# Rotation product, row statistics, gate and scatter of the first expert layer in one stage

## The reference

```python
x = x + _L0_gnn_ref(_layernorm(x), edge_weight, src, dst)   # layernorm(x) @ m, m = product of 100000 rotations
x = x + _L0_ffn_ref(_layernorm(x)[None], gate_w, gate_b, w1, b1, w2, b2)[0]

# in _L0_ffn_ref, with 8 experts and room for C = 977 rows in each:
logits = x @ gate_w + gate_b
probs = softmax(logits); idx = argmax(probs); prb = probs[idx]
pos = (cumsum(one_hot(idx)) * one_hot(idx)).sum(-1) - 1      # place in the expert's room
buf = zeros((E, C, D)).at[idx, where(pos < C, pos, C)].set(x, mode='drop')
```

## Time and profile before

| | us |
|---|---|
| median of 3 runs (7909.3 to 7910.01) | 7909.55 |
| the profiled execution, its time | 7921.19 |
| the profiled execution, its span | 7919.4 |
| busy in the span: PE / DVE / ACT / POOL | 5157.7 / 3609.7 / 3195.4 / 4682.5 |
| mean granted clock of TensorE, share of full speed | 0.743 |

### The profile page before, as it was taken

One profiled execution on the slowest core, in us unless ns is written; L12 is line 12 of the kernel. 1 busy time (PEld: TensorE's weight loads), 2 busy tenths in 40 slices (PEclk: granted clock), 3 DMA queues, 4 the chain that ended last, 5 costly groups with the idle time before them and its releaser, 6 DMA issues. The chain is left out here.

```text
span 7919.4 us, 115948 instructions
## 1 busy us (share of the span) xinstructions
PE 5157.7 (65%) x22196; PEld 4061.3 (51%) x22197; DVE 3609.7 (46%) x8810; ACT 3195.4 (40%) x8284; POOL 4682.5 (59%) x4875
## 2 busy tenths in 40 slices
PE   2689867777645555779734344566677566676796
PEld 2566544454434444579734344345456345455795
DVE  7634467777820000453500000466666566667533
ACT  2533244444343433333333333244444344444432
POOL 5032277777567777125277777677774777773253
PEclk9779977777777777779755555577778777777698
DMA  2432144444233333222311111344443344442324
GB/s 61 176 78 83 48 120 117 115 117 116 83 100 108 109 109 108 66 78 70 100 28 28 28 28 26 91 115 115 115 114 83 103 115 115 114 114 66 106 69 137
DMA packets 417887, 726.44 MB, mean 92 GB/s; under 512 B 129365, under 2 KB 278315, under 8 KB 414167
## 3 DMA queue, kind: packets, MB, share of 16 engines
q0 software_dynamic: 208256, 503.58, 23.6%
q1 hardware_dynamic: 202475, 208.74, 8.5%
q10 hardware_dynamic: 6508, 8.01, 0.3%
HBM read 596.63 MB, written 123.54 MB: 91 GB/s over the span
## 5 line engine op out<-in xcount | busy, mean ns | idle before, releaser
L1017 POOL DMA_INDIRECT g_rows<-table,src_idx x2326 | 2218.0, 954 | 710.0 <-issue 709.4
L1292 PE MATMUL g_p_win<-g_rows,g_hot 128*128 128x264 f32 (+1 forms) x4704 | 1502.2, 477 | 44.5 <-issue 41.4
L1292 PEld LDWEIGHTS g_p_win<-g_rows,g_hot 128*128 128x128 f32 x4704 | 1069.1, 238 | 305.3 <-issue 94.0
L1182 ACT ACTIVATE g_hot<-iota,near 128x128 f32<-128x128 f32 x2352 | 720.7, 386 | 411.7 <-PE g_p_win L1292 375.7
L1017 POOL DMA_INDIRECT g2p_rows<-rows,src_idx x771 | 736.3, 955 | 235.2 <-issue 235.2
L1017 POOL DMA_INDIRECT gcnp_rows<-table,src_idx x771 | 734.8, 953 | 235.5 <-issue 235.5
L1098 DVE TENSOR_TENSOR g_rows<-g_rows,g_p_w 128x1792 f32<-128x1792 f32 x336 | 679.0, 2021 | 27.0 <-ACT g_rows L1210 2.7
L1201 ACT ACTIVATE g_resets_f<-fwd_reset 128x112 f32 (+3 forms) x168 | 54.8, 326 | 1176.1 <-DVE g_b L1069 1061.3
L1249 PE MATMUL g_p_turn<-slide,g_a 128*8 128x128 f32 (+1 forms) x168 | 59.0, 351 | 715.6 <-DVE g_a L1057 715.6
L1105 DVE TENSOR_TENSOR agg<-agg,g2p_p_out 128x256 f32 x112 | 42.1, 417 | 943.3 <-PE g2p_p_out L1254 943.3
L1105 DVE TENSOR_TENSOR agg<-agg,gcnp_p_out 128x64 f32 x112 | 20.3, 221 | 957.0 <-PE gcnp_p_out L1254 957.0
(11 more groups left out here) (831 smaller groups left out, 10986.2 us busy)
## 6 DMA issues: line engine op xcount, KB each, us to landing
g_stage<-table SPq DMA_DIRECT2D x3328, 1.0 KB
g_rows<-table,src_idx POOLq DMA_INDIRECT x2326
g2p_stage<-rows SPq DMA_DIRECT2D x1664, 1.0 KB
gcnp_stage<-table SPq DMA_DIRECT2D x1664, 0.2 KB
back<-agg SPq DMA_DIRECT2D x7, 1792.0 KB, 34.9
rows<-r_row SPq DMA_DIRECT2D x98, 128.0 KB, 3.0
gcn_row_in<-back SPq DMA_DIRECT2D x14, 896.0 KB, 7.3
c_row<-back SPq DMA_DIRECT2D x14, 896.0 KB, 13.5
```

The lines of the kernel that those rows point to most:

```text
L1017: gp.indirect_dma_start(rows[:, s, j, 0:width + H], None, table, bass.IndirectOffsetOnAxis(g.src_idx[:, at:at + 1], 0)).then_inc(got[s], 16)
L1182: last = nc.scalar.activation(hot[:, j, :], g.iota[:, :], ACT.Square, scale=-1.0, bias=g.near[:, bass.ds(c * J + j, 1)])
L1292: last = nc.tensor.matmul(p_win[:, 0:W], hot[:, j, :], rows[:, s, j, :], start=(j == 0), stop=(j == J - 1))
```

## The change

`x_plus_product` and `front` are gone. One function, `product_front`, does the work of both in a single stage. `STEPS` is 61 and the loops run over t from 0 to 66. In step t an engine works at tile t of the product and at tile t - 12 (`LAG`) of the gate. Statistics become `GroupNorms`: scale and shift are worked out for each group of seven tiles (six DVE instructions "spread", a square root on ACT "root", two DVE instructions "fit"), since the gate part needs them while the product goes on. The turned tile of the gate part is copied from PSUM to `rt` by DVE, no longer by ACT. The PSUM buffers `p_x`, `p_r` and `p_pos` are single, `out` and `p_log` double. `first` and `tmp` become double. `g.mt` moves from a buffer of its own into a part of `agg` that lies behind `row`. The sum of the counts, the penalties and everything behind the stage are unchanged. `room_known` stands on ACT before the first tile of the product.

```diff
-def x_plus_product(nc, g, name, rhs, bias=None):
...
-def front(nc, g, name, w, bias, top2, softmax, prefetch, room_known=None):
+def product_front(nc, g, name, rhs, w, bias, prefetch, room_known):
+    NG, LAG = NT // GROUP, 12
...
+        p_x, p_r = ph.ps("p_x", [P, 2, P]), ph.ps("p_r", [P, 2, P])
+        out = [ph.ps(f"out{s}", [P, D]) for s in range(2)]
+        norms = GroupNorms(nc, g, ph)
+        STEPS = NT + LAG
+        ending = lambda t, after: (t - after) % GROUP == GROUP - 1 and 0 <= t - after < NT
+        group_of = lambda t, after: (t - after) // GROUP
+        CHOOSE, COUNT, PLACE = LAG + 1, LAG + 3, LAG + 4
...
             @block.scalar
+                def feed(t):
+                    if t >= 2:
+                        ac.wait_ge(fed_turned, t - 1)
+                    normalised(nc, g, xn[:, t % 2, :], t).then_inc(fed, 1)
+                def copy_fed(t):
+                    ac.wait_ge(fed_turned, t + 1)
+                    if t >= 2:
+                        ac.wait_ge(summed, t - 1)
+                    nc.scalar.activation(xt[:, t % 2, :, :], p_x[:, :, :], ACT.Identity).then_inc(fed_copied, 1)
+                room_known(ac)
+                feed(0)
+                feed(1)
+                copy_fed(0)
+                for t in range(STEPS + 6):
+                    if t + 2 < NT:
+                        feed(t + 2)
+                    if 0 <= t - LAG + 2 < NT:
+                        normalise(t - LAG + 2)
+                        if (t - LAG + 2) % GROUP == 0:
+                            name_rows((t - LAG + 2) // GROUP)
+                    if t + 1 < NT:
+                        copy_fed(t + 1)
+                    if ending(t, CHOOSE + 1):
+                        exps(group_of(t, CHOOSE + 1))
+                    if ending(t, 1):
+                        norms.root(ac, group_of(t, 1))
             @block.tensor
+                def turn_fed(t):
+                    pe.wait_ge(fed, t + 1)
+                    if t >= 1:
+                        pe.wait_ge(fed_copied, t)
+                def product(t):
+                    pe.wait_ge(fed_copied, t + 1)
+                    if t >= 2:
+                        pe.wait_ge(added, t - 1)
+                def turn(t):
+                    pe.wait_ge(normal, t + 1)
+                    if t >= 1:
+                        pe.wait_ge(copied, t)
...
+                turn_fed(0)
                 pe.wait_ge(loaded, 32)
                 pe.wait_ge(tri_ready, 2)
+                for t in range(STEPS + 6):
+                    if t + 1 < NT:
+                        turn_fed(t + 1)
+                    if t < NT:
+                        product(t)
+                    if 0 <= t - LAG + 1 < NT:
+                        turn(t - LAG + 1)
+                    if 0 <= t - LAG < NT:
+                        multiply(t - LAG)
+                    if ending(t, COUNT):
+                        positions(group_of(t, COUNT))
             @block.vector
+                def take(t):
+                    x = g.x[:, t, :]
+                    dv.wait_ge(summed, t + 1)
+                    V.tensor_tensor(x, x, out[t % 2][:, :], ALU.add).then_inc(added, 1)
+                    dv.wait_ge(added, t + 1)
+                    norms.tile(t)
+                def copy(t):
+                    dv.wait_ge(turned, t + 1)
+                    if t >= 2:
+                        dv.wait_ge(multiplied, t - 1)
+                    V.tensor_copy(rt[:, t % 2, :, :], p_r[:, :, :]).then_inc(copied, 1)
...
+                for t in range(STEPS + 6):
+                    if 0 <= t - LAG < NT:
+                        copy(t - LAG)
+                    if t < NT:
+                        take(t)
+                    if ending(t, 0):
+                        norms.spread(dv, group_of(t, 0))
+                    if ending(t, 2):
+                        norms.fit(dv, group_of(t, 2))
+                    if ending(t, CHOOSE):
+                        choose(group_of(t, CHOOSE))
+                    if ending(t, PLACE):
+                        put_group(group_of(t, PLACE))
...
-        front(nc, g, "r0", a["L0_ffn_gate_w"], a["L0_ffn_gate_b"], False, True, wt.first_two, lambda gp: gp.wait_ge(g.filled, 16 * g.fills))
+        product_front(nc, g, "r0", g.mt, a["L0_ffn_gate_w"], a["L0_ffn_gate_b"], wt.first_two, lambda eng: eng.wait_ge(g.filled, 16 * g.fills))
...
-        g.mt = sb("mt", [P, 2, D])
+        g.mt = g.agg_wide[:, :, :].rearrange("p t w -> p (t w)")[:, NT * RW:NT * RW + 2 * D].rearrange("p (k d) -> p k d", k=2)
-        x_plus_product(nc, g, "l0g", g.mt[:, :, 0:D])
```

More of the change, by code:

```diff
@@ L2162, in name_rows @@
                         ac.wait_ge(ops, 1)
[L2163 to L2169, removed]
+                    nc.scalar.activation(row[:, n, :, D:D + 1].rearrange("p t a -> p (t a)"), ids[:, tiles_of(n)], ACT.Identity).then_inc(named, 1)
@@ L2195, in _ @@
                 mm = nc.tensor.matmul
+                def turn_fed(t):
+                    pe.wait_ge(fed, t + 1)
+                    if t >= 1:
+                        pe.wait_ge(fed_copied, t)
+                    for k in range(2):
+                        last = nc.tensor.transpose(p_x[:, k, :], xn[:, t % 2, k * P:(k + 1) * P], g.ident[:, :])
+                    last.then_inc(fed_turned, 1)
+                def product(t):
+                    pe.wait_ge(fed_copied, t + 1)
+                    if t >= 2:
+                        pe.wait_ge(added, t - 1)
+                    for k in range(2):
+                        last = mm(out[t % 2][:, :], xt[:, t % 2, k, :], rhs[:, k, :], start=(k == 0), stop=(k == 1))
+                    last.then_inc(summed, 1)
                 def turn(t):
@@ L2285, in _, with put_group @@
+                    V.tensor_tensor(tmp[:, s, :, :], sc, over_e(best[:, gs]), ALU.subtract).then_inc(less, 1)
+                def put_group(n):
+                    s, last, gs = n % 2, n == NG - 1, tiles_of(n)
                     dv.wait_ge(counted, n + 1)
[L2286 to L2288 removed]
+                    where = by_tile(p_pos[:, :, :])
+                    ch.do(V.tensor_scalar(over[:, :, :], where, CAP - 0.5, OUT, ALU.is_ge, ALU.mult))
@@ L2289, in _ @@
                     ch.do(V.tensor_tensor(place[:, :, :], where, region[:, :, :], ALU.add))
-                    if not top2:
-                        ch.do(V.tensor_tensor(place[:, :, :], place[:, :, :], over[:, :, :], ALU.add))
-                    for k, chosen_one in enumerate((first, second)[:K]):
-                        ch.do(V.tensor_tensor(eq[:, :, :], chosen_one[:, :, :], place[:, :, :], ALU.mult))
-                        ch.do(V.tensor_reduce(out=slot[:, :], in_=eq[:, :, :], axis=AX.X, op=ALU.add))
-                        if last:
-                            ch.do(V.tensor_tensor(slot[:, :], slot[:, :], invalid[:, :], ALU.add))
-                        V.tensor_copy(put[:, k, gs], slot[:, :]).then_inc(put_ready, 1)
-                        dv.wait_ge(put_ready, K * n + k + 1)
@@ L2299, in _ @@
[L2299 to L2305 removed]
+                    ch.do(V.tensor_tensor(place[:, :, :], place[:, :, :], over[:, :, :], ALU.add))
@@ new lines, in put_group @@
+                    ch.do(V.tensor_tensor(eq[:, :, :], first[:, s, :, :], place[:, :, :], ALU.mult))
+                    ch.do(V.tensor_reduce(out=slot[:, :], in_=eq[:, :, :], axis=AX.X, op=ALU.add))
+                    if last:
+                        ch.do(V.tensor_tensor(slot[:, :], slot[:, :], invalid[:, :], ALU.add))
+                    V.tensor_copy(put[:, gs], slot[:, :]).then_inc(put_ready, 1)
+                    dv.wait_ge(put_ready, n + 1)
+                    dv.wait_ge(exped, n + 1)
```

191 lines of the change are left out of this document (49 added, 142 removed).

## The result

| | before | after |
|---|---|---|
| median, us | 7909.78 (7909.14 to 7913.7, 6 runs) | 7940.73 (7934.13 to 7944.05, 6 runs) |
| ratio after to before | | 1.0037, 95% interval 1.0024 to 1.005 |
| the profiled execution's span, us | 7919.4 | 7942.1 |
| next stage's first load (SP, `e_xin`), us from the span's start | 477.12 | 508.74 |

The change makes the kernel 31 us slower, 0.4%. I had said 7934, 24.6 us slower. The stretch that the change touches is 31.6 us longer; behind it both kernels do the same, and the profiled execution of before happened to lie above its median there. They took 23 us more than the kernel before beside them, so the loss is 23 to 31 us.

A forecast was written before the change was run, and what follows sets the result against it. Before, PE bounds the product stage and, at 1.2 GHz, is busy through most of the gate stage. 362.6 + 95.9 + 20.9 + 0.3 + 22.0 = 501.7 against 477.1, 24.6 us longer: 7934 us, range 7904 to 7958.

The forecast's parts named there:

- The head: Stage start: ACT waits for the DRAM-table clears, so work starts at 345.4 instead of 317.0, 28.4 us lost.
- Steps with the product alone: First 12 tiles, before gate work: 1.9 us to the first product plus 15.3 us, as before.
- Mixed steps: 37 tiles, t = 12 to 48, product and gate together: PE and DVE wait in turn, 95.9 us.
- I take 18%: Mixed steps: share of time with TensorE at 1.2 GHz, from a later stage, raising 90.9 to 95.9 us.
- Steps with the gate alone: Last 12 tiles: 15.6 us at 1.3 each, plus one choose, put, fit and positions, 5.3; together 20.9 us.
- The end: Last choose to the next stage's first load: 22.0 us instead of 24.1, as the scatter queue is gone.
- ACT and its tables: Merged stage: ACT doesn't bind; ten more table loads, 1.28 us each, cost nothing, falling where PE waits for choose or put.
- Rival 1: Mixed steps: DVE and PE run past each other, only DVE's queue counts, 74 us; 7907 in all; chance 0.16.
- Rival 2: Head: the clears land sooner and are no wait, 28.4 us less, 7906 alone; chances 0.05, 0.04 with Rival 1.
- rival 3: Mixed steps: TensorE stays at 1.2 GHz, 128 us instead of 95.9, 7966 in all; chance 0.08.
- my own case: Merged stage: PE and DVE wait for each other in a loop, from +8 to +42 us; chance 0.62.
- Rival 4: Merged stage: ACT's table loads are not covered, 19 us more, 7953 in all; chance 0.05.

The follow-up runs named there:

- e1: Changed kernel with only ACT's wait for the DRAM-table clears moved from the first tile to its first write into row (t = 10): 7939.86 us.
- e2: As e1, with PE's and DVE's waits for the gate weights also moved to their first use: 7927.17 us.
- e3: Changed kernel with the exponential of the scores replaced by a plain copy, removing 10 of 11 table loads: 7940.26 us.
- e5: Changed kernel with the second copies (p_r to rt) back on ACT instead of DVE: 7914.04 us.
- e9: e5 with the exponential of the scores replaced by a plain copy, as in e3: 7907.54 us.
- e4: Changed kernel with DVE's choose and put cut into pieces of two instructions, exponential, positions and put one or two steps later: 7920.69 us.
- e8: Changed kernel with the pieces of e4, the moved waits of e2, and the gate part 19 tiles behind instead of 12: 7896.29 us.
- e6: Changed kernel with unread matmuls on PE, 5 behind the product at choose and 4 at put: 7932.81 us.

## Why the prediction was right, point by point

**The head.** Predicted 28.4 us lost, start at 345.4; it was 27.7 and 344.69. The load of the gate weights, which I took as hidden, is a gate of its own (e1), 1 us behind the clears; it cost next to nothing in after, where the first product started at 347.55 and I had 347.3. What I hadn't seen is that half of the loss would stay with the wait at its first real use (e2), because of ACT's queue.

**Steps with the product alone.** First mixed step predicted at 362.6; the first product followed by transposes of the gate side starts at 362.07.

**Mixed steps.** This term was too small: 95.9 us predicted, 101 measured (362.1 to DVE's last addition at 463.19). Of its parts, the plain step was 1.75 and measured 1.70, and the reason given for it was wrong: I had PE and DVE wait for each other in a loop, and the trace shows PE without a gap and DVE waiting. That the number came near is luck, since PE's own work alone came to 1.67. The bursts were right in place: choose takes 2.4 us on DVE (399.04 to the copy at 401.46), and PE stands for 2.13 of it. What failed is "I take 18%" of the time at 1.2 GHz, from the earlier trace rows. It was 46% in after (0.77 from 363 to 453); but the same mixed part had 0.89 and 0.85, 22% and 30%, in e1 and e3, and took 97 to 98 us there:

```profile
363.00:453.00 90.00, 73.07 (x432) 62.30 (x432) 60.97 (x218) 60.75 (x128) 23.71 (x25) 0.89 0.17 60
```

So this share isn't one number for this kernel, and mine lay below all three. The 0.29 in the sum isn't explained in the prediction; it fits 1 - 2.46 / 3.45, the part by which a tile is shorter at the full clock. With 46% the sum would have given 105. Some of the difference to 101 comes from put: at 1.2 GHz PE is busy with the product through most of it (to 412.53, where put ran from 410.99 to 412.80) and stops for 0.80 us, where e1 at the full clock had 1.91, as predicted. So "PE idle over 2 us behind every choose and put" was right for choose alone. The group period was 20.4 in the profile and 18.8 to 20.5 in e1 and e3, and the 17 to 19 that I had named holds for three of the eight groups of e1 and e3 and for none of after; PEclk, which I had put at 0.8 to 1, was outside in after and inside in the other two.

**Steps with the gate alone.** 20.9 and 0.3 predicted, 23.3 measured (463.19 to the last choose at 486.53), and 23.3 in e1 and e3 too. A step took 1.27 at 1.2 GHz, where I had 1.3. The fault is in the count: with `PLACE` at t = `LAG` + 4 behind a group's last tile, puts fall at t = 22, 29, 36 and 43 in the mixed part and at 50 and 57 here, and the sum has one here, six in all for seven groups. The missing one, 1.9 in the prediction's own price, is about the 2.1 that this term is short. The two puts, and PE's wait for DVE's copy behind each:

```profile
467.87 0.22 DVE L2265 TENSOR_SCALAR r_over<-r_p_pos 128x56 f32<-128x56 f32 x1 [0.92 <-PE r_p_pos L2190]
...
470.22 0.66 PE L2172 MATMUL r_p_r<-slide,agg 128*128 128x128 f32 x2 [1.36 <-DVE r_rt L2236]
...
480.67 0.22 DVE L2265 TENSOR_SCALAR r_over<-r_p_pos 128x56 f32<-128x56 f32 x1 [1.16 <-PE r_p_pos L2190]
...
483.01 0.66 PE L2172 MATMUL r_p_r<-slide,agg 128*128 128x128 f32 x2 [1.29 <-DVE r_rt L2236]
```

(One `positions`, at t = 49, also belongs here and not in the mixed part, where the sum has five; that moves 0.4 from one term to the other.) **The end:** 22.0 predicted, 22.2 measured (508.74 - 486.53).

**ACT and its tables.** Cost at nothing was right (e3). It holds only while another stop covers the loads; in e5 that cover is gone, and e9 shows the price, 5 to 6.5 us. The Trainium skill (ScalarE: Activation LUTs, What ACT_TABLE_LOAD costs) gives a drain of about 1.38 us with each switch. The traces here show none. After has, on ACT's timeline:

```profile
403.90 0.38 ACT L2112 ACTIVATE r_xt<-r_p_x 128x256 f32<-128x256 f32 x1 [1.08 <-PE r_p_x L2155]
404.30 1.28 ACT L478 ACT_TABLE_LOAD   x1
405.60 0.30 ACT L478 ACTIVATE r_g_std<-r_g_var,r_g_eps 128x7 f32<-128x7 f32 x1
```

The load starts 0.02 us behind the copy's end, and the root starts 0.02 us behind the load: 1.28 us is all. It is the same for the exponential where it waits for nothing else (e5: load at 393.90, exponential at 395.21).

**The rivals.** Rival 1 (only DVE's queue counts, a group of 14.0) didn't happen, and e4 shows why: it needs DVE's work in pieces, and then a group does take 14.9. Rival 2 (the clears are no wait) and rival 3 (1.2 GHz throughout) are out by the rows above; the truth lay between 3 and my own case, nearer to my own. Rival 4 is out by e3. The missing 7 us of the profile are the mixed part (5, by the clock) and the put left out of the count (2); in e1 and e3 some 3 us were missing, of which the mixed part is 1 to 2.

**What was luck.** The sign rested on the head, which was read to within 1 us. From the head's end to the next stage's first load I had 156.3 us (501.7 - 345.4) against 160.1 before (477.12 - 317.0), so a merged stage 4 us faster than the two apart. It was 160 (e3) to 164 (after), so level with the two or 4 us slower. On the work itself the prediction named the wrong side, by 4 to 8 us, and the loss of 28 us ahead of it kept that from showing in the sign.

**Where the gain of merging went.** With the copies left on ACT the merged stage needs 134.7 us from ACT's first tile to the next stage's first load (478.77 less 344.07, in e5), where the two stages took 160.1 (477.12 less 317.0). So merging is worth 25 us. The copies by DVE take all of it back (508.74 - 344.69 = 164.0 in after, 160 in e3), and the wait at the head, 28 us, is then the loss. The copies were undone by themselves (e4, e5). The head was undone by itself only in part, 13 us (e2); that the rest is in ACT's wait at t = 10 is what its 12.11 us there show, and with the longer lag of e8, on top of the pieces, 7.6 us more came back.

## What to carry to other kernels

A copy that PE waits for should not stand behind a long burst in the queue of the engine that makes it: either cut the burst into short pieces, or give the copy to an engine without bursts, even if that makes it the busiest one (with the copies ACT was busy 95% of the time, and the kernel faster than with the copies on DVE at 64%). When two stages are merged, every wait at the head of the second becomes a wait of the first; move each to its first use, all of them together, and look at what is queued behind that use. A cost that is "covered" is covered by something: when the covering stop is removed, price it again.

## What the runs showed that I had not expected

- A stop of TensorE of 2.1 us in a stretch that is otherwise busy without a gap was followed by 9 us at 1.2 GHz (0.50 from 402 to 411). In the mixed part of e4 and e5, with stops of at most 1.0 and 1.3 us, the clock was 1.00. In after it is so in each group with a choose (0.74 to 0.76 in each stretch of 20 us from 378 on). It isn't a fixed price: in e1 the stop behind the first choose, 2.13 us as well, was followed by a clock of 1.00 up to 391, and the low stretch came only behind that of the put after it, 1.91 us (0.66 from 391 to 396). Why the same stop has it at one time and not at another stays open. The work behind the stop was gapless, and still slow.
- Nine matmuls a group that nobody reads (e6) kept the clock at 1.00 and made a group 1 to 3 us shorter; of the kernel's time that is 3 to 8 us.
- The length of this clock's low stretch differs between executions: groups of 18.8 to 20.5 us in kernels with the same mixed part, which is the spread of 4 us in the next stage's start (504.38, 504.92, 508.74).
